# Attention loop of a graph network layer: the vector engine's first additions of exponentials moved to two pairs of DMAs, and the maxima one step further ahead

## What is computed

```python
q = (x @ Wq + bq).reshape(N, H, HEAD)
k = (x @ Wk + bk).reshape(N, H, HEAD)
v = (x @ Wv + bv).reshape(N, H, HEAD)
scores = jnp.einsum('nhd,mhd->nhm', q, k) / np.sqrt(HEAD)
adj = jnp.zeros((N, N), jnp.float32).at[edge_index[0], edge_index[1]].set(1.0)
scores = jnp.where(adj[:, None, :] == 0, -1000000000.0, scores)
attn = jax.nn.softmax(scores, axis=1)
attn_out = jnp.einsum('nhm,mhd->nhd', attn, v).reshape(N, D_OUT)
```

## Time and profile before

| | us |
|---|---|
| median of 3 runs | 479.39 (478.98 to 479.75) |
| the profiled execution, its own time | 479.94 |
| its span in the profile | 478.1 |
| PE busy in the span | 449.8 (94%) |
| DVE busy | 316.5 (66%) |
| ACT busy | 190.2 (40%) |
| POOL busy | 162.7 (34%) |
| mean granted clock of TensorE | 0.988 of full |

### The profile page before, as it was taken

One profiled execution on the slowest core, in us unless ns is written; L12 is line 12 of the kernel. 1 busy time (PEld: TensorE's weight loads), 2 busy tenths in 40 slices (PEclk: granted clock), 3 DMA queues, 4 the chain that ended last, 5 costly groups with the idle time before them and its releaser, 6 DMA issues.

```text
span 478.1 us, 5890 instructions
## 1 busy us (share of the span) xinstructions
PE 449.8 (94%) x2075; PEld 328.1 (69%) x2075; DVE 316.5 (66%) x581; ACT 190.2 (40%) x264; POOL 162.7 (34%) x106
## 2 busy tenths in 40 slices
PE   3999999798899998799999999999999999999996
PEld 2455634343458886678778788888888888888764
DVE  5999858899997986958764944433272237133854
ACT  4878825446214421252543353034403242237230
POOL 3000131112141997348240444243344334344100
PEclk9999999989999999889999999999999999999999
DMA  8760000000021233103102223323220342120002
GB/s 273 188 257 1 1 1 1 22 1 0 1 95 61 88 112 129 70 0 129 71 1 88 88 89 88 89 85 113 89 89 5 96 155 81 39 88 1 0 1 88
DMA packets 22475, 34.35 MB, mean 72 GB/s; under 512 B 5680, under 2 KB 5936, under 8 KB 22448
## 3 DMA queue, kind: packets, MB, share of 16 engines
q1 hardware_dynamic: 22160, 33.85, 21.4%
q10 hardware_dynamic: 288, 0.13, 0.1%
HBM read 32.93 MB, written 1.05 MB: 71 GB/s over the span
## 4 chain that ended last, share of the span: by engine, by line
PE 72%; DVE 18%; issue 4%; ACT 3%; DMA 1%; POOL 1%; SPq 0%; POOLq 0%; DVEq 0%
PE ps L1203 15%; PE ps L1205 15%; PE ps L1204 15%; PE ps L1276 6%; PE ps L1265 4%; PE ps L1232 3%; PE ps L1231 3%; PE ps L1258 3%; DVE rsum L919 2%; DVE e_sb L381 1%; DVE stats L735 1%; PE ps L1348 1%; DMA x_sb<-in_x 1%; PE ps L1370 1%; PE ps L1216 1%
## 5 line engine op out<-in xcount | busy, mean ns | idle before, releaser
L460 POOL TENSOR_TENSOR w_lo<-w_stage,w_hi 128x1024 fp32r<-128x1024 f32 x22 | 53.5, 2434 | 130.2 <-ACT w_hi L541 119.5
L541 ACT ACTIVATE w_hi<-w_stage 128x2048 fp32r<-128x2048 f32 x23 | 43.9, 1909 | 61.8 <-PE ps L1205 61.8
L461 POOL TENSOR_TENSOR w_lo<-w_stage,w_hi 128x1024 fp32r<-128x1024 f32 x22 | 57.3, 2604 | 0.0
L1203 PE MATMUL ps<-w_hi,hid_hi 128*128 128x512 f32 x128 | 49.9, 390 | 0.5 <-DVE hid_lo L1114 0.5
L1205 PE MATMUL ps<-w_hi,hid_lo 128*128 128x512 f32 x128 | 49.8, 389 | 0.0
L1204 PE MATMUL ps<-w_lo,hid_hi 128*128 128x512 f32 x128 | 49.8, 389 | 0.0
L1203 PE MATMUL ps<-T_hi,w_hi 128*128 128x512 f32 (+1 forms) x112 | 41.0, 366 | 0.4 <-POOL w_lo L461 0.4
L1204 PE MATMUL ps<-T_lo,w_hi 128*128 128x512 f32 (+1 forms) x112 | 40.2, 359 | 0.0
L1205 PE MATMUL ps<-T_hi,w_lo 128*128 128x512 f32 (+1 forms) x112 | 40.2, 359 | 0.0
L1112 DVE TENSOR_SCALAR tmp<-ps,bl 128x512 f32<-128x512 f32 x16 | 12.0, 750 | 39.9 <-ACT hid_hi L686 39.9
L806 DVE TENSOR_SCALAR one_src<-iota_n,edge_m,edge_w 128x256 f16 x128 | 34.2, 340 | 0.0
(11 more groups left out here) (214 smaller groups left out, 996.6 us busy)
## 6 DMA issues: line engine op xcount, KB each, us to landing
w_stage<-in_L_gnn_Wr SPq DMA_DIRECT2D x8, 1024.0 KB, 5.3
w_stage<-in_L_gnn_Wl SPq DMA_DIRECT2D x8, 1024.0 KB, 5.4
w_stage<-in_L_gnn_W SPq DMA_DIRECT2D x5, 1024.0 KB, 6.8
x_sb<-in_x SPq DMA_DIRECT2D x4, 256.0 KB, 3.7
w_q<-in_L_gnn_Wq SPq DMA_DIRECT2D x1, 1024.0 KB, 7.9
w_k<-in_L_gnn_Wk SPq DMA_DIRECT2D x1, 1024.0 KB, 10.2
w_v<-in_L_gnn_Wv SPq DMA_DIRECT2D x1, 1024.0 KB, 5.7
w_o<-in_L_gnn_Wo SPq DMA_DIRECT2D x1, 1024.0 KB, 8.9
```

The source lines that it names most:

```text
L460: gp.tensor_tensor(w_lo[s][:, 0:2], stage[s][:, 0:2], f32(w_hi[s][:, 0:2]), ALU.subtract)
L461: gp.tensor_tensor(w_lo[s][:, 2:4], stage[s][:, 2:4], f32(w_hi[s][:, 2:4]), ALU.subtract)\
L541: nc.scalar.activation(w_hi[u % 2][:], stage[u % 2][:], ACT.Copy).then_inc(hi_made, 1)
L1203: nc.tensor.matmul(goal, a_hi, b_hi, start=start, stop=False, **kw)
```

## The change

In steps 2 to 7 the first additions of the exponentials are done by DMAs. A new tile `pair_sum` (128 x 4 x 256) takes the place of `pool_sum`. For each group g of a step, SP issues a DMA that copies the group's first two heads from `e` to its half of `pair_sum`, once `exp_done` says that this group is there and `pairs_read` that the step before has been read. When that copy has landed (`pair_copied`), POOL issues a DMA with `accum_op=ALU.add` that adds the group's other two heads to it (`pair_added`). Both move 256 KB. DVE waits for both additions, adds the halves of `pair_sum` (L921 in the changed file) into `half_sum`, adds the last two halves into `rsum`, and goes on as before.

The rest of the change:

- DVE: the maxima stand two steps ahead of the sums (those of steps 3 and 4 behind a reciprocal), `values_in(3)` behind the sums of step 1, and the products of steps 0 to 5 are one instruction of eight heads.
- PE: values(i - 3) in place of values(i - 2) in the loop; what is left of them follows the loop, with the first product with `w_o` between.
- ACT: `attended_out(0)` a step later.
- Four buffers of exponentials in place of three.
- SP's 12 copies stand behind the load of W1B and ahead of the rows B2 and GAMMA2.

```diff
@@ -101,7 +101,7 @@
     k_sb = place("k_sb", [P, PAIRS, N], F32, rQK + MAT)
     v_sb = place("v_sb", [P, NT, D], F32, rQK + 2 * MAT)
     half_sum = place("half_sum", [P, HEADS // 2, HN], F32, rQK + 3 * MAT)
-    pool_sum = place("pool_sum", [P, HEADS // 4, HN], F32, rQK + 3 * MAT + 4 * HN * 4)
+    pair_sum = place("pair_sum", [P, HEADS // 2, HN], F32, rQK + 3 * MAT + 4 * HN * 4)
     ff_hi = place("ff_hi", [P, FT, N], F32R, rQK)
     ff_lo = place("ff_lo", [P, FT, N], F32R, rQK + 2 * MAT)
     R_hi = place("R_hi", [P, NT, D], F32R, rQK)
@@ -111,7 +111,7 @@
 
 
 
-    E_BUFS = 3
+    E_BUFS = 4
     e_bufs = [place(f"e_sb{i}", [P, HEADS, HN], F32, rVZ + i * MAT) for i in range(E_BUFS)]
     c_hi = place("c_hi", [P, NT, N], F32R, rVZ)
     c_lo = place("c_lo", [P, NT, N], F32R, rVZ + MAT)
@@ -280,7 +280,8 @@
         ct_ready = sem("ct_ready")
         T_made = sem("T_made")
         edges_whole = sem("edges_whole")
-        sums_made, rinv_made, pool_half = sem("sums_made"), sem("rinv_made"), sem("pool_half")
+        sums_made, rinv_made, pairs_read = sem("sums_made"), sem("rinv_made"), sem("pairs_read")
+        pair_copied, pair_added = [sem(f"pair_copied{g}") for g in range(2)], [sem(f"pair_added{g}") for g in range(2)]
         dve = sem("dve")
         pool = sem("pool")
         ln_var = sem("ln_var")
@@ -428,6 +429,14 @@
                 if u >= 2:
                     sp.wait_ge(lo_made, u - 1)
                 sp.dma_start(stage[u % 2][:], src).then_inc(stage_in[u % 2], 16)
+                if u == W1B:
+                    for step in range(DIRECT, STEPS):
+                        for g in range(2):
+                            sp.wait_ge(exp_done, 2 * step + g + 1)
+                            if step > DIRECT:
+                                sp.wait_ge(pairs_read, step - DIRECT)
+                            sp.dma_start(pair_sum[:, 2 * g:2 * g + 2], e_bufs[step % E_BUFS][:, 4 * g:4 * g + 2])\
+                              .then_inc(pair_copied[g], 16)
                 for i in ahead.get(u, []):
                     load_row(i)
                 if u in (WN, WC):
@@ -494,11 +503,10 @@
             gp.wait_ge(sums_made, 1)
             split_lo_tile(W1A, DT - 1)
             for i in range(DIRECT, STEPS):
-
-                e = e_bufs[i % E_BUFS]
-                gp.wait_ge(exp_done, 2 * i + 1)
-                gp.wait_ge(sums_made, i)
-                gp.tensor_tensor(pool_sum[:], e[:, 0:2], e[:, 2:4], ALU.add).then_inc(pool_half, 1)
+                for g in range(2):
+                    gp.wait_ge(pair_copied[g], 16 * (i - DIRECT + 1))
+                    gp.dma_start(pair_sum[:, 2 * g:2 * g + 2], e_bufs[i % E_BUFS][:, 4 * g + 2:4 * g + 4],
+                                 accum_op=ALU.add).then_inc(pair_added[g], 16)
             gp.wait_ge(sums_made, STEPS)
             add_row(BO, 1, h_sb, bo_added)
             gp.wait_ge(prob_done, 2 * STEPS)
@@ -628,7 +636,7 @@
                     coarse_scores(1, 0)
                 if DIRECT <= i + 1 < STEPS:
                     coarse_scores(i + 1, 1)
-                if i == NT + 1:
+                if i == NT + 2:
                     attended_out(0)
                 if i + 2 < STEPS:
                     coarse_scores(i + 2, 0)
@@ -898,28 +906,37 @@
             maxima(0)
             for i in range(STEPS):
                 e = e_bufs[i % E_BUFS]
-                if 1 <= i < STEPS - 1:
-                    maxima(i + 1)
                 if i == 1:
-                    values_in(3)
-                v.wait_ge(exp_done, 2 * (i + 1))
+                    maxima(2)
+                if DIRECT < i < STEPS - 2:
+                    maxima(i + 2)
                 r = rsum[:, i % 2, :]
                 if i < DIRECT:
+                    v.wait_ge(exp_done, 2 * (i + 1))
                     link(nc.vector.tensor_tensor(half_sum[:], e[:, 0:4], e[:, 4:8], ALU.add))
                     link(nc.vector.tensor_tensor(half_sum[:, 0:2], half_sum[:, 0:2], half_sum[:, 2:4], ALU.add))
                 else:
-                    link(nc.vector.tensor_tensor(half_sum[:, 0:2], e[:, 4:6], e[:, 6:8], ALU.add))
-                    v.wait_ge(pool_half, i - DIRECT + 1)
-                    link(nc.vector.tensor_tensor(half_sum[:, 0:2], half_sum[:, 0:2], pool_sum[:], ALU.add))
+                    for g in range(2):
+                        v.wait_ge(pair_added[g], 16 * (i - DIRECT + 1))
+                    nc.vector.tensor_tensor(half_sum[:, 0:2], pair_sum[:, 0:2], pair_sum[:, 2:4], ALU.add)\
+                      .then_inc(pairs_read, 1)
+                    v.wait_ge(pairs_read, i - DIRECT + 1)
                 nc.vector.tensor_tensor(r, half_sum[:, 0], half_sum[:, 1], ALU.add).then_inc(sums_made, 1)
                 if i == 0:
                     maxima(1)
                     values_in(2)
+                if i == 1:
+                    values_in(3)
                 v.wait_ge(sums_made, i + 1)
                 nc.vector.reciprocal(r, r).then_inc(rinv_made, 1)
+                if i in (1, 2):
+                    maxima(i + 2)
                 v.wait_ge(rinv_made, i + 1)
-                probabilities(nc.vector, i, slice(0, HEADS // 2)).then_inc(prob_done, 1)
-                probabilities(nc.vector, i, slice(HEADS // 2, HEADS)).then_inc(prob_done, 1)
+                if i < STEPS - 2:
+                    probabilities(nc.vector, i, slice(0, HEADS)).then_inc(prob_done, 2)
+                else:
+                    probabilities(nc.vector, i, slice(0, HEADS // 2)).then_inc(prob_done, 1)
+                    probabilities(nc.vector, i, slice(HEADS // 2, HEADS)).then_inc(prob_done, 1)
 
 
             g1_row, be1_row = wait_row(GAMMA1), wait_row(BETA1)
@@ -1376,29 +1393,29 @@
             scores(0, 1)
             values_part(2, 1, 2)
             for i in range(STEPS):
-                if i == STEPS - 1:
-
-                    pe.wait_ge(raw_in["o"], 16)
-                    pe.wait_ge(exp_done, 2 * STEPS - 2)
-                    plain_rows_tile(wo_bank(0), 0, att_sb, w_o, wo_done)
                 centre(i, 0)
                 centre(i, 1)
                 if i == 0:
                     scores(1, 0)
                 if i == 1:
                     values_part(3, 0)
-                if i >= 2:
-                    values(i - 2, 0)
+                if i >= 3:
+                    values(i - 3, 0)
                 if i + 1 < STEPS:
                     scores(i + 1, 1)
-                if i >= 2:
-                    values(i - 2, 1)
+                if i >= 3:
+                    values(i - 3, 1)
                 if i + 2 < STEPS:
                     scores(i + 2, 0)
                 if i == 0:
                     values_part(2, 3)
                 if i == 1:
                     values_part(3, 1, 2, 3)
+            values(STEPS - 3, 0)
+            values(STEPS - 3, 1)
+            pe.wait_ge(raw_in["o"], 16)
+            pe.wait_ge(exp_done, 2 * STEPS - 2)
+            plain_rows_tile(wo_bank(0), 0, att_sb, w_o, wo_done)
             values(STEPS - 2, 0)
             values(STEPS - 2, 1)
             plain_rows_tile(wo_bank(1), 1, att_sb, w_o, wo_done)
```

## The result

The changed kernel takes 488.64 us (488.56 to 490.5, 4 runs) against 479.19 us (478.71 to 479.75, 4 runs) for the kernel before, run in the same way: a ratio of 1.0198, with a 95% interval of 1.018 to 1.0215. It is 9.4 us slower. I had forecast 483.0 us, slower by 3.6 us: the right side, and less than half of the loss. The time lies inside the range that I gave, 477.6 to 490.0 us, near its upper end.

The account below looks back on a forecast made before the run. It took DVE's work in the attention loop as the bound; 2.4 us lost at the start, 1.8 in the steady steps waiting for DMAs, less 0.55 at the end, made 3.6 us slower, 483.0 us, range 477.6 to 490.0.

Follow-up runs that it names:

- e5: The changed kernel with two buffers of pair_sum and PE's two products with w_o ahead of the products of steps 5 and 6 with v: 478.04 us.
- e1: The changed kernel without its DMAs, POOL and DVE adding as before the change, its order, four buffers and single product kept: 481.45 us.
- e4: The changed kernel with POOL's DMAs overwriting pair_sum instead of adding to it, DVE adding 1.0 in its read, output differing: 478.63 us.
- e3: The changed kernel with SP loading the row B2 ahead of the copies instead of behind them: 492.82 us.

## What to carry to other kernels

A single buffer that DMAs fill and an engine reads in each step made a closed chain here: its period was issue, landing, second issue, second landing and read, though DVE stood idle for part of it, and a second buffer took 8.8 us off. That is the first thing to try. An operation whose price no row shows should be bounded by its traffic as well as by its neighbours' landing times, and work moved past a loop must be added up as a list from its last wait to the end. Before handing work to another unit, look for what moves within the lists alone: two moves gave 2.9 us here, more than the 1.4 us of e5, in which the DMAs are waited for only at step 2 (1.20 us). No run put hidden DMAs beside the order of before, whose change cost 1.7 us in e1, so what the DMAs alone can give stays open.

## What the runs showed of the hardware that I had not expected

- Additions by DMA within SBUF, 256 KB each in rows of 2 KB a partition, went at some 190 to 200 GB/s in the change; plain copies in the same steps at 350 to 400. Issue to landing 3.8 against 2.3 to 2.4 us in the median. POOL was busy 0.86 to 1.13 us with issuing an addition, and 0.54 to 0.72 us with a plain copy (e4).
- The granted clock of a stretch 50 us behind a change differed (1.00 before, 0.88 after), though the instructions and the idle time ahead of them (1.97 us) are the same. What decided it is open.
- A load of 256 KB from HBM, issued 0.4 us ahead of the copies within SBUF, made these 3.6 us long in place of 2.3 (e3, step 2).
